# Small-row products of a transformer block: 2, 48 and 16 rows padded to 128 with zeros

## The reference

```
q = x @ Wq.T + bq; k = x @ Wk.T + bk; v = x @ Wv.T + bv
...
return y @ Wo.T + bo
...
y = jax.nn.gelu(jnp.einsum('bsd,edf->bsef', x, g) + gb, approximate=False)
y = y * (jnp.einsum('bsd,edf->bsef', x, w1) + b1)
return jnp.einsum('bsef,efd->bsed', y, w2) + b2
...
aff = jax.nn.sigmoid(jnp.einsum('bsd,de->bse', x, wa))
topk_p, topk_i = jax.lax.top_k(aff, K)
```

## Time and profile before

| | |
|---|---|
| median of 3 runs | 1911.63 us (1911.61 to 1915.59) |
| profiled execution, first to last instruction (span) | 1892.8 us |
| what lies around the span, median less span | 18.8 us |
| PE busy | 1604.0 us, 85% of the span |
| PEld / DVE / ACT / POOL busy | 968.4 / 889.3 / 771.4 / 466.1 us |
| TensorE clock, mean share of full | 0.879 |

### The profile page before, as it was taken

One profiled execution on the slowest core, in us unless ns is written; L12 is line 12 of the kernel. 1 busy time (PEld: TensorE's weight loads), 2 busy tenths in 40 slices (PEclk: granted clock), 3 DMA queues, 4 the chain that ended last, 5 costly groups with the idle time before them and its releaser, 6 DMA issues. The chain is left out here.

```text
span 1892.8 us, 22807 instructions
## 1 busy us (share of the span) xinstructions
PE 1604.0 (85%) x6687; PEld 968.4 (51%) x6687; DVE 889.3 (47%) x2070; ACT 771.4 (41%) x2026; POOL 466.1 (25%) x653
## 2 busy tenths in 40 slices
PE   3478998989999898989575999997999999999930
PEld 3354554655555455654344878885444444444410
DVE  2345466665657667566444532222322323232249
ACT  2256567666667666667422111111212222222213
POOL 0112122231323232231210122221222222222246
PEclk8668697988979797997767999998999999999965
DMA  3445445474655456364334467754576766555468
GB/s 123 50 79 97 102 103 138 111 161 107 168 130 135 119 130 157 89 153 98 121 111 161 146 226 239 260 199 156 134 202 177 201 143 169 137 142 113 72 220 340
DMA packets 123601, 280.15 MB, mean 148 GB/s; under 512 B 18932, under 2 KB 45046, under 8 KB 116600
## 3 DMA queue, kind: packets, MB, share of 16 engines
q1 hardware_dynamic: 106984, 241.07, 44.3%
q0 software_dynamic: 16496, 37.63, 10.2%
HBM read 256.74 MB, written 109.61 MB: 194 GB/s over the span
## 5 line engine op out<-in xcount | busy, mean ns | idle before, releaser
L1279 DVE TENSOR_REDUCE mr<-bank 128x1 f32<-128x512 f32 (+3 forms) x352 | 217.7, 634 | 173.4 <-PE bank L1822 170.1
L1941 PE MATMUL bank<-ring,xg 128*128 x632 | 285.1, 594 | 0.0
L1084 ACT ACTIVATE P<-bank 128x512 f32<-128x512 f32 x320 | 189.4, 596 | 218.1 <-PE bank L1836 217.1
L1067 ACT ACTIVATE bank<-bank,mr 128x384 f32<-128x384 f32 (+3 forms) x512 | 256.4, 503 | 24.0 <-DVE mr L1279 24.0
L1820 PE MATMUL bank<-Ks,Qs 96*128 96x384 f32 (+3 forms) x512 | 183.2, 412 | 56.1 <-DMA Qs<-st 33.5
L1836 PE MATMUL bank<-Qs,Ks 98*128 98x512 f32 x320 | 169.9, 537 | 27.6 <-ACT P L1084 23.6
L1756 PE MATMUL bank<-xt,ws 128*128 128x512 f32 x768 | 182.4, 394 | 3.8 <-DMA xt<-xt_scratch 3.8
L1663 POOL TENSOR_SCALAR_AFFINE_SELECT P<-P 128x256 f32<-128x256 f32 (+1 forms) x192 | 92.6, 486 | 366.7 <-ACT P L1084 365.9
L1820 PEld LDWEIGHTS bank<-Ks,Qs 96*128 96x128 f32 x512 | 103.7, 218 | 149.9 <-issue 47.8
L1941 PEld LDWEIGHTS bank<-ring,xg 128*128 128x128 f32 x632 | 114.3, 191 | 114.6 <-issue 114.6
L1756 PEld LDWEIGHTS bank<-xt,ws 128*128 128x128 f32 x768 | 145.8, 190 | 36.5 <-DMA xt<-xt_scratch 4.7
(11 more groups left out here) (221 smaller groups left out, 2377.1 us busy)
## 6 DMA issues: line engine op xcount, KB each, us to landing
ring<-in_w SPq DMA_DIRECT2D x79, 1024.0 KB
ring<-in_w SPq DMA_DIRECT2D x79, 512.0 KB
Qs<-st SPq DMA_DIRECT2D x192, 128.0 KB, 4.8
xs<-xs_scratch SPq DMA_DIRECT2D x79, 258.0 KB, 3.9
xs_scratch<-xs_scratch SPq DMA_DIRECT2D x78, 258.0 KB, 4.4
xt<-xt_scratch SPq DMA_DIRECT2D x32, 512.0 KB, 6.6
xs<-xn_scratch SPq DMA_DIRECT2D x64, 256.0 KB, 3.0
xt_scratch<-xt SPq DMA_DIRECT2D x30, 512.0 KB, 3.4
```

The source lines that it names most:

```text
L1067: m = e.activation(ps[:, o * k:o * k + k], ps[:, o * k:o * k + k], ACT.Exp, scale=-1.0, bias=mr[:, G % 2, c:c + 1], accum_out=se[:, G % 2, ...
L1084: e.activation(Pt[:, p, :], bank[PA.bank[step]][:, :], ACT.Exp, scale=-1.0).then_inc(s_exp, 1)
L1279: e.tensor_reduce(mr[:, G % 2, 0:16].rearrange("p (h i) -> p h i", i=4)[:, h:h + n, i:i + 1], bank[PA.bank["max", b, p, j]][:, 0:n * k].re ...
L1941: e.matmul(ps[:, :].rearrange("p (o n) -> p o n", o=1), xg[:, q, 128 * k:128 * k + 128], ring[:, bass.ds(reg[n], 1), 512 * k:512 * k + 512 ...
```

## The change

All these small products get operands of 128 rows. `ones`, `bv_s`, `bo_s`, `rb_s`, `ohj` and `lg` become 128 partitions high; rows that hold no bias are zero, and the row count of a product is 128. The transposition of the logits takes all 128 rows of `lg` and the full identity, so it also moves 128 columns and writes 128 columns where it moved 16 and wrote 16. Five memsets are added on DVE or moved there, with a semaphore `pad_dve`, on which ACT's first writes of these tiles wait.

```diff
-        ones = ctx.enter_context(nc.sbuf_tensor("ones", [2, 128], F32R))
+        ones = ctx.enter_context(nc.sbuf_tensor("ones", [128, 128], F32R))
...
-            lg = sb("lg", [16, 2, 128])
+            lg = sb("lg", [128, 2, 128])
...
-            bv_s = sb("bv_s", [2, 128], F32R)
+            bv_s = sb("bv_s", [128, 128], F32R)
...
-            bo_s = sb("bo_s", [2, 512], F32R)
+            bo_s = sb("bo_s", [128, 512], F32R)
...
-            rb_s = sb2("rb_s", [48, 512], F32R)
+            rb_s = sb2("rb_s", [128, 512], F32R)
...
-            ohj = sb2("ohj", [48, 2, 128], F32R)
+            ohj = sb2("ohj", [128, 2, 128], F32R)
...
                 w.wait_ge(dve_ld, minus)
+                w.wait_ge(pad_dve, 2)
                 e.activation(dst[0:2, :], q, ACT.Copy).then_inc(act_ld, 1)
...
-                    e.activation(lg[:, n % 2, :], bank[PA.bank[("rt", *a)]][0:E, 0:128], ACT.Copy).then_inc(lg_act, 1)
+                    w.wait_ge(pad_dve, 4)
+                    e.activation(lg[0:16, n % 2, :], bank[PA.bank[("rt", *a)]][0:E, 0:128], ACT.Copy).then_inc(lg_act, 1)
...
+            w.wait_ge(pad_dve, 5)
             e.activation(b2_s[:, :], wst[0:80, 512:1024], ACT.Copy).then_inc(b_act, 1)
-            e.activation(rb_s[:, :], wst[0:48, 0:512], ACT.Copy).then_inc(b_act, 1)
+            e.activation(rb_s[0:48, :], wst[0:48, 0:512], ACT.Copy).then_inc(b_act, 1)
...
+            e.memset(bv_s[:, :].bitcast(F32), 0.0).then_inc(pad_dve, 1)
+            e.memset(bo_s[:, :].bitcast(F32), 0.0).then_inc(pad_dve, 1)
+            e.memset(mr[:, :, :], 1.0).then_inc(pad_dve, 1)
+            e.memset(lg[:, :, :], 0.0).then_inc(pad_dve, 1)
             e.memset(ones[:, :].bitcast(F32), 1.0).then_inc(dve_const, 1)
             e.memset(Ks[96:98, :, :, :].bitcast(F32), -1.0).then_inc(dve_const, 1)
-            e.memset(mr[:, :, :], 1.0).then_inc(dve_const, 1)
...
+            e.memset(rb_s[:, :].bitcast(F32), 0.0).then_inc(pad_dve, 1)
             e.tensor_tensor(comb[:, :, :], oh[:, 0, :, :], pwb(0), ALU.mult).then_inc(dve_own, chain.up())
...
-                    m = e.matmul(ps, ones[0:2, :], bv_s[0:2, :], start=False, stop=True)
+                    m = e.matmul(ps, ones[:, :], bv_s[:, :], start=False, stop=True)
...
-                        e.matmul(ps, ones[0:2, :], bo_s[0:2, :], start=False, stop=True).then_inc(wo_pe, 1)
+                        e.matmul(ps, ones[:, :], bo_s[:, :], start=False, stop=True).then_inc(wo_pe, 1)
...
-                    e.transpose(bank[PA.bank[step]][:, 0:E], lg[:, nth("lg", a) % 2, :], ident[0:E, 0:E]).then_inc(lgT_pe, 1)
+                    e.transpose(bank[PA.bank[step]][:, 0:128], lg[:, nth("lg", a) % 2, :], ident[:, :]).then_inc(lgT_pe, 1)
```

More of the change, by code:

```diff
@@ L495, in program @@
         pool_const = sem("pool_const")
+        pad_dve = sem("pad_dve")
         dve_const = sem("dve_const")
@@ L1201, in _ @@
             e.tensor_tensor(bv_q, bv_a, row_[:, 0:128], ALU.subtract).then_inc(dve_ld, 1)
+            e.memset(bv_s[:, :].bitcast(F32), 0.0).then_inc(pad_dve, 1)
+            e.memset(bo_s[:, :].bitcast(F32), 0.0).then_inc(pad_dve, 1)
+            e.memset(mr[:, :, :], 1.0).then_inc(pad_dve, 1)
+            e.memset(lg[:, :, :], 0.0).then_inc(pad_dve, 1)
             e.memset(ones[:, :].bitcast(F32), 1.0).then_inc(dve_const, 1)
             e.memset(Ks[96:98, :, :, :].bitcast(F32), -1.0).then_inc(dve_const, 1)
-            e.memset(mr[:, :, :], 1.0).then_inc(dve_const, 1)
-            w.wait_ge(dve_const, 3)
+            w.wait_ge(dve_const, 2)
+            w.wait_ge(pad_dve, 3)
             def rope_first(pa, ra, ba, tab_, n, waits_for):
```

## The result

| | median | runs | ratio to before, 95% interval |
|---|---|---|---|
| before | 1913.61 us | 1911.61 to 1916.41 | |
| with the change | 1849.51 us | 1843.81 to 1853.91 | 0.969, 0.965 to 0.973 |
| again, later, before | 1904.75 us | 1894.72 to 1921.21 | |
| again, later, with the change | 1852.84 us | 1847.21 to 1868.06 | 0.9713, 0.9673 to 0.9754 |

The change is 2.9 to 3.1% faster, 52 to 64 us by the medians. The span of the profiled execution went from 1892.8 to 1849.1 us, 43.7 us. The new runs list their spans too: time less span is 1.7 us in each.

What follows compares the result with a forecast made beforehand. PE was taken to bound the routed stage and most of attention. Routed -26.1, attention -11.7 and memsets +0.9 gave -36.9 us, so 1874.7 us, with an 8-in-10 range of 1853 to 1889.

Steps and rivals of the forecast that it cites:

- The stall and its cause: PE finishes what is in the array between few-row and many-row products; 80 rows or more count as many.
- Rival 4: No stall goes, padding changes nothing in loading ahead; only memsets are left: 1912.5 us, chance 0.03.
- Rival 3: The stall belongs to the change from float32 to float32r, so the routed stage keeps it: 1900.8 us, chance 0.04.
- The routed term: Routed bias products: 0.33 us saved in each of 79 slots, 26.1 us, all of it counted.
- The memsets: Added DVE memsets at the program's start, ahead of PE's first work: 0.9 us lost.
- The attention term: Value bias, output bias and logits' transposition: 19.5 us less PE work, six tenths of it counted, 11.7 us.
- the six stretches: Attention's half-clock stretches before the change, one per batch in six batches: 24 us long, each costing 7 us.
- The base: Starting time for the sum: profiled span 1892.8 us plus 18.8 us taken to lie around it in the median.
- Rival 1: Attention's waits for ACT's exponentials take all of its saving: 1886.4 us, chance 0.14.
- Rival 2: Denser PE work keeps the clock up in attention's half-clock stretches: about 1833 us for six, 1861 for two; chance 0.07.
- The sign against me: Half-clock stretches other than the six seen before the change would show the prediction wrong; no size given.
- Rival 5: Slower: PE waits longer for ACT in attention and its clock falls more often; 1931 us with eight falls, chance 0.03.

Runs made afterwards that it cites:

- 64-row run: The changed kernel with the routed bias product over 64 rows and attention's products few-rowed as before the change: 1901.87 us in one run.

## Why the prediction was right and where it was wrong

**The stall and its cause** were read rightly: few rows next to many, on both sides of the product, 80 as good as 128. The 64-row run puts the step where only a rule had put it. That rule is the one of the Trainium skill, "TensorEngine Tiling (Array Packing)", "Key Properties", that a change of the tiling mode drains the engine; the page has modes of 32, 64 and 128 rows. The trace agrees, with 6.38 us per slot at 48 and 64 rows and 6.04 at 80 and 128. That the array is emptied is seen in no row; what the rows show is a load that is not done ahead. The other rule, of the Trainium skill, "TensorE: Matmul & The Clock Gate", "Part 3: Packing small matmuls", that a load overlaps only with another row group, is not borne out as I used it: the padded load comes 0.43 us behind the one before it. The same part of the page also lets a load into the background weight buffer go ahead of running products, which I had left out. Rival 4 fell with the measurement. Rival 3 (data kind) fell too: more rows of the same kind take the stall away.

**The routed term**, 79 x 0.33 = 26.1 us, measured 26.6 us by runs and 26.2 in the profiles. Counting all of it was right, for PE waits for nothing there.

**The memsets**, 0.9 us: PE's first transposition starts 1.1 us later (30.1 and not 29.0), and the run with memsets alone can't be told from before. The memset of `ones` stands among them too, but it took its time before as well.

**The attention term was mis-sized**: 11.7 us, six tenths of 19.5, where the runs gave 23.6 by itself, and 30 for the value bias alone (20 to 38 by the interval), more than the 8.5 us of its stalls. Two steps failed. First, "six tenths" spread over all three edits. The value bias counts in full, at full clock 9.6 - 8.5 = 1.1 us a batch in the value step, 8.8 in eight batches, close to my 8.5. PE goes from this step to the keys without a wait, so nothing absorbs it there. The output bias shows little or no gain (4 us alone with an interval of 0 to 15, and nothing beside the value bias), and neither does more work taken out (the run without bias products). Where its saving goes is not shown. PE's waits of attention (64 to 985 us) for the transfer of `Qs` are, in before,

```profile
PE bank L1820 <- DMA Qs<-st: 33.5, 8, 23.3
```

in the change,

```profile
PE bank L1829 <- DMA Qs<-st: 37.6, 10, 23.3
```

and with no bias products at all:

```profile
PE bank L1828 <- DMA Qs<-st: 40.3, 10, 23.4
```

which is 4 and 7 us more. But over all profiles this wait is 33.2 to 37.2 us with the value bias stalling and 32.9 to 40.3 without, so three of them don't show that it takes the gain back.

Second, I took the clock for a rival (0.07) when it was part of the change's effect. I had looked at the six stretches at a fixed place and not at the value steps, which ran at half clock in two of the seven batches behind the first. The two steps at half clock fell from 14.8 and 16.1 us to 8.1 and 8.5 in the profiled pair, 14.3 us, of which some 3 are stalls (a step wholly at half clock takes 17.5 us with them and 16.0 without). In the medians the half-clock time fell by 26 to 40 us wherever the value bias lost its stalls, and stayed at 459 to 473 wherever it did not, save for the one kernel with 451 in a single run. Over all runs of the same kernel, 10 us less at half clock go with about 3 us less time (a line fitted within kernels, 0.33; the rows at either clock had given 7 us for 24, 0.29). So some 33 us less are worth about 11. With 8.5 of stalls that makes 20 of the 24 to 30 us.

The profiles give a second estimate. I fitted the 98 distances from one batch's first value product to the next one's (14 kernels, 7 distances each, with a length of its own for each batch). A microsecond at half clock adds 0.39 us, and a stalling value bias adds 1.2 us a batch beside it, with an error of 0.3. That is 10 us of stalls in eight batches and 13 for 33 us less at half clock, 23 of the 24 to 30. If the output bias is put into the fit, padding it saves nothing (0.7 us more a batch, with an error of 0.4), and the value bias has 1.6 us a batch. The rest lies within the intervals. Why there is less half-clock time behind the second batch stays open.

**The base.** I made the sum against 1892.8 + 18.8. The 18.8 us were not a fixed part around the span (that is 1.7 us) but the distance of one short execution to the median of others. It changed nothing in the sum, which is one of differences. But attention in the trace of before was shorter than it mostly is: it ended at 1004.6 us there and at 1033.9 and 1027.7 in the profiles with the tiles alone and the routed product alone, whose attention has the same stalls. Of the value steps that can go at half clock, it showed two where others show up to five.

**The rivals and the signs.** Rival 1 (waits take all) fell, for attention gained as much as the routed stage, though for the output bias alone the runs look like it. Rival 2 (the clock) came true in part, and not as I had priced it. The sign against me, other half-clock stretches than the six, did show: where before has six of 24 us, the change has 24, 17, 17, 24, 17 and 14 us, from 292 to 846 us. Rival 5, a clock that falls more often, was right to be set low: in sum it went the other way. PE's waits for ACT in the four largest groups grew from 78 us (64 to 1000 us, before) to 83 (64 to 985, the change), within the 8 that I had named.

## What to carry to other kernels

Look for the few-row product in the weight loads, not in the products: a load that starts together with its own product, with a long idle before it, beside neighbours that are loaded ahead. If it sums over at most 64 partitions between products of more, give it 80 or 128 with zeros; ask of each such place whether PE goes on behind it without a wait, as in the value step and the routed slot. Here only those two gave back their stalls measurably. And where the clock changes level inside a dense piece of work, a small stall in that piece may cost several times its length (6.7 us for 1.1 us of stalls in the second batch); compare kernels by their granted clock before crediting a gain to an edit.

## What the runs showed of the hardware that I had not expected

- A load and a product over 64 rows stall beside 128-row ones as those over fewer do (a routed slot takes 6.38 us at 48 and 64 rows, a value step 9.6 us at 2 and 64). Over 80 rows they don't (6.04 us a slot, as at 128).
- Four stalls in a value step of some 8 us, 0.28 us each (9.6 less 8.5 us over four), go with a fall of TensorE's clock from 2.4 to 1.2 GHz in the midst of it, in the second batch of every kernel in the table that has them (14.5 to 14.8 us for the step, seven kernels); without them it holds in all seven (7.7 to 8.1 us). That the engine was busy by its records (15.35 of 16 us) did not keep the clock up. In the change the fall comes behind the step instead (0.53 from 138 to 146 us).
- Executions of one and the same kernel on one core differ by 26 us of 1905 (1894.72 to 1921.21), and their mean clocks from 0.870 to 0.887.
- A padded bias product's record starts 0.03 us behind the product before it and is 0.80 us long, while the product behind it starts 0.64 later: such a record's start does not give the pace, the starts around it do.
